# A long convolution beside an attention: pair products made by GpSimd in the loop of the first attention, half of the query products on GpSimd, expert weights loaded in the convolution

## The reference, cut to what matters

```python
x = x + _L0_attn_ref(_layernorm(x, axis=-1), ...)
x = x + _L0_xattn_ref(ctx_2048, ctx_2048, _layernorm(x, axis=-1), L0_xattn_ssm_kernel, L0_xattn_D, 8)
x = x + _L0_ffn_ref(...)        # mixture of experts
...
def _L0_xattn_ref(k, v, q, ssm_kernel, D, head_dim):
    ...
    kv = jnp.einsum('bhil,bhjl->bijhl', k_, v_)
    kv_f = jnp.fft.rfft(kv, n=fft_size)
    kernel_f = jnp.fft.rfft(ssm_kernel, n=fft_size)
    y = jnp.fft.irfft(kv_f * kernel_f, n=fft_size)[..., :L]
    out = y + kv * D[None, None, None, :, None]
    out = jnp.einsum('bijhl,bhil->bjhl', out, q_)
```

## Time and profile before

| | us |
|---|---|
| median of 3 runs | 718.73 (716.68 to 723.39) |
| the profiled execution | 719.01 |
| its span, first to last instruction | 716.8 |
| first attention, tiles 6 to 13 | 8.95 for each tile (two in 17.91) |
| convolution, VectorE's first product to the end of its last sum | 172.84 to 246.19, 73.35 |

### The profile page before, as it was taken

How to read it: one execution, slowest core, us unless ns; L and a number is a source line. 1 busy time by engine, 2 the same in 40 slices (tenths; PEclk the granted TensorE clock), 3 DMA queues, 4 the chain that set the end, 5 groups by cost and what they waited for, 6 DMA issues and landing times.

```text
span 716.8 us, 16348 instructions
## 1 busy us (share of the span) xinstructions
PE 611.1 (85%) x4646; PEld 462.3 (65%) x4647; DVE 535.8 (75%) x1217; ACT 389.6 (54%) x796; POOL 320.4 (45%) x672
## 2 busy tenths in 40 slices
PE   6999999987888899988999777999999577637776
PEld 5788888864444575566777566888888433225554
DVE  4789999975999985324222688999999668689994
ACT  2667777762111133144332264777777458869993
POOL 1223222254999443611111554333333368566772
PEclk9999999999999999999999998999999869959999
DMA  8912400001333000274541212000000000000001
GB/s 293 416 61 64 139 0 0 0 2 21 57 56 57 15 1 15 104 243 126 156 129 51 59 39 111 2 1 0 0 0 2 2 0 0 0 0 1 32 29 59
DMA packets 27343, 42.00 MB, mean 59 GB/s; under 512 B 3521, under 2 KB 22609, under 8 KB 26401
## 3 DMA queue, kind: packets, MB, share of 16 engines
q1 hardware_dynamic: 23808, 31.14, 14.5%
q0 software_dynamic: 3488, 10.28, 4.2%
HBM read 31.15 MB, written 10.26 MB: 58 GB/s over the span
## 4 chain that ended last, share of the span: by engine, by line
PE 44%; DVE 18%; issue 18%; ACT 7%; POOL 5%; DMA 4%; DVEq 1%; SPq 1%; POOLq 0%; ACTq 0%
PE ps L1121 5%; PE ps L325 4%; PE ps L710 4%; PE ps L353 4%; DVE work L542 3%; PE ps L363 3%; DVE work L548 2%; PE ps L1129 2%; PE ps L373 2%; PE ps L335 2%; DVE wide L557 2%; POOL sorted_x L1182 2%; PE ps L314 2%; DMA small<-hank 2%; ACT work L1716 2%
## 5 line engine op out<-in xcount | busy, mean ns | idle before, releaser
L230 POOL TENSOR_TENSOR var_eps<-mv,powers 128x1 f32<-128x1 f32 x80 | 16.9, 211 | 199.1 <-DVE mv L221 199.1
L470 ACT COPY wide<-ps 128x512 f32<-128x512 f32 x128 | 75.6, 593 | 44.9 <-PE ps L325 42.8
L542 DVE TENSOR_REDUCE work<-ps 128x8 f32<-128x1024 f32 x64 | 77.8, 1216 | 7.1 <-PE ps L314 6.5
L325 PE MATMUL ps<-ident,work 128*128 128x128 f32 x512 | 76.8, 283 | 6.0 <-DVE work L571 3.9
L465 ACT ACTIVATE work<-work 128x1024 f32<-128x1024 f32 x64 | 68.4, 1068 | 23.2 <-DVE work L548 22.7
L548 DVE TENSOR_TENSOR work<-ps,work 128x1024 f32<-128x1024 f32 x64 | 77.8, 1216 | 0.6
L325 PEld LDWEIGHTS ps<-ident,work 128*128 128x128 f32 x512 | 59.8, 145 | 22.8 <-issue 16.7
L710 PE MATMUL ps<-ctxT,small 128*128 128x512 f32 (+1 forms) x192 | 65.3, 492 | 8.1 <-DMA small<-hank 3.0
L710 PEld LDWEIGHTS ps<-ctxT,small 128*128 128x128 f32 x192 | 35.3, 190 | 37.5 <-issue 28.5
L1155 DVE TENSOR_TENSOR work<-work,ps 128x256 f32<-128x256 f32 x23 | 9.7, 421 | 57.2 <-ACT work L1149 57.1
L353 PE MATMUL ps<-xnT,w_qkv 128*128 128x128 f32 x256 | 38.3, 296 | 16.5 <-DVE work L548 14.4
(11 more groups left out here) (207 smaller groups left out, 1553.3 us busy)
## 6 DMA issues: line engine op xcount, KB each, us to landing
wide<-in_expert_gu SPq DMA_DIRECT2D x1, 4096.0 KB, 22.3
small<-hank SPq DMA_DIRECT2D x32, 128.0 KB, 3.8
sorted_x<-small POOLq DMA_DIRECT2D x1, 2944.0 KB, 12.0
work<-sorted_x SPq DMA_DIRECT2D x23, 128.0 KB, 2.1
sorted_y<-work POOLq DMA_DIRECT2D x23, 128.0 KB, 2.2
xn_all<-in_ctx_rev_t SPq DMA_DIRECT2D x1, 2048.0 KB, 10.6
wide<-in_expert_d SPq DMA_DIRECT2D x1, 2048.0 KB, 26.5
xn_all<-in_ffn_w SPq DMA_DIRECT2D x2, 1024.0 KB, 6.3
```

Source lines behind the costliest of these rows:

```text
L325: mm = pe.transpose(T[r % 2][:, h * P:(h + 1) * P], prob[r][:, h * P:(h + 1) * P], ident)
L470: act.copy(probT[r], T[r % 2]).then_inc(s["pT"], 1)
L542: dve.tensor_reduce(mxs[:, 8 * g:8 * g + 8], S2[g], AX.X, ALU.max).then_inc(s["mx"], 1)
```

## The change: what it does

1. The pair products of a head are made by two instructions for both halves together (128x1024 and 128x512) in place of four (two 128x512, two 128x256).
2. Eleven of the 16 heads get them during the first attention: head 10 in body 5, heads 9 to 2 in bodies 6 to 13 (`"ahead"`, first thing in GpSimd's body), heads 0 and 1 in bodies 14 and 15 as before. They lie in the part of `wide` that held expert weights, in `ctx_sb` and in `ctxT`. The other five (11 to 15) are made in the convolution, after heads 1, 3, 5, 7 and 11.
3. ScalarE copies the mirrored quarter and the lower part out of PSUM (two copies for each half), and GpSimd multiplies both with the queries in one 128x512 instruction (`pool_rest`). VectorE's 128x256 product (line 816) goes; its 128x512 product and its sum stay.
4. The Toeplitz matrices have four buffers in place of two.
5. The expert weights are loaded by SP in the convolution: the first 4 MB once 12 heads are through TensorE and the load of the last Toeplitz matrix is issued, the other 2 MB after 15 heads. The wait of TensorE for them moves behind routing and shared experts.

```diff
@@ pool_body
+                if layer == 0:
+                    follow("pool", pool, t, u, "ahead")
                 if there(t):
                     pool.wait_ge(f.xn, f.base + t + 1)
...
+        AGAIN = {11: 0, 12: 1, 13: 2, 14: 3, 15: 10}
...
+            in_wide = lambda n: wide[:, n * KV:(n + 1) * KV]
+            kv = {0: ctxT[:, 0:KV], 1: ctxT[:, 2048:2048 + KV], 10: ctx_sb[:, 2048:2048 + KV]}
+            kv.update({h: in_wide(9 - h) for h in range(2, 10)})
+            kv.update({h: kv[free] for h, free in AGAIN.items()})
...
+                if name == "pool" and step == "ahead" and not isinstance(t, int):
+                    pool_pairs(eng, 15 - t, wide[:, ds((t - 6) * KV, KT * UPPER)],
+                               wide[:, ds((t - 6) * KV + KT * UPPER, KT * LOWER)])
@@ sync
+                with sp.Fori(1, CH // 4) as i:
+                    for k in range(4):
+                        h = 4 * i + k
+                        sp.wait_ge(s["conv"], 4 * (h - 3))
+                        load_toep(sp, h, k)
...
+                sp.wait_ge(s["conv"], 4 * 10)
+                sp.dma_start(w_ex_gu, cp(a["expert_gu"])).then_inc(moe_loaded, 16)
+                sp.wait_ge(s["conv"], 4 * 15)
+                sp.dma_start(w_ex_d, cp(a["expert_d"])).then_inc(moe_loaded, 16)
@@ scalar
+                act.copy(into[:, :, :, 0:LO], upper[:, :, LO:CD, :]).then_inc(s["rest_sb"], 1)
+                act.wait_ge(s["conv"], 4 * h + 2 * lt + 2)
+                act.copy(into[:, :, :, LO:CD], lower).then_inc(s["rest_sb"], 1)
@@ gpsimd
+            def pool_early(pool, t):
+                head = {5: 10, NB - 2: 0, NB - 1: 1}
+                if t in head:
+                    pool_kv(pool, head[t])
...
+            def pool_rest(pool, h, lt):
+
+                pool.wait_ge(s["rest_sb"], 4 * h + 2 * lt + 2)
+                pool.wait_ge(s["sum"], 2 * h + lt + 1)
+                pool.tensor_tensor(products(lt)[:, :, LO:CD, :],
...
             def gpsimd(pool):
+                late = {1: 11, 3: 12, 5: 13, 7: 14, 11: 15}
                 pool.wait_ge(f.xnT, f.base_T + NB)
+                for h in range(CH):
+                    pool_rest(pool, h, 0)
+                    pool_rest(pool, h, 1)
+                    if h in late:
+                        pool.wait_ge(s["conv"], 4 * (AGAIN[late[h]] + 1))
+                        pool_kv(pool, late[h])
@@ dve_prod
-                dve.wait_ge(s["conv"], 4 * h + 2 * lt + 2)
-                dve.tensor_tensor(products(lt)[:, :, LO:CD, LO:CD],
...
```

More of the change, by code:

```diff
@@ L660, in convolution @@
             s = {k: sem(f"conv_{k}") for k in (
-                "toep0", "toep1", "kv", "conv", "quarter_sb", "quarter", "prod", "sum")}
+                "toep0", "toep1", "toep2", "toep3", "kv", "conv", "rest_sb", "rest", "prod", "sum")}
             LO = CD // 2
             UPPER, LOWER = NB * LO * CD, NB * LO * LO
-            kv = [kt_x(ctxT[:, u * 2048:u * 2048 + KT * (UPPER + LOWER)], UPPER + LOWER) for u in range(2)]
-            quarter = [xnT[:, lt * D:(lt + 1) * D] for lt in range(2)]
+            KV = KT * (UPPER + LOWER)
+            rest = [xnT, xn]
+            in_wide = lambda n: wide[:, n * KV:(n + 1) * KV]
+            kv = {0: ctxT[:, 0:KV], 1: ctxT[:, 2048:2048 + KV], 10: ctx_sb[:, 2048:2048 + KV]}
+            kv.update({h: in_wide(9 - h) for h in range(2, 10)})
+            kv.update({h: kv[free] for h, free in AGAIN.items()})
             toep = [kt_x(small[:, 800 + u * 512:800 + (u + 1) * 512], D) for u in range(2)]
+            toep += [kt_x(w_qkv[0][:, u * 512:(u + 1) * 512], D) for u in range(2)]
             prod = [ctx_sb[:, u * 1024:(u + 1) * 1024] for u in range(2)]
@@ L676, in beside @@
                         front_xn(eng, f, n, 1 - u)
-                if name == "pool" and there(n):
+                if name == "pool" and step == 0 and there(n):
                     front_rstd(eng, f, n, 1 - u)
+                if name == "pool" and step == "ahead" and not isinstance(t, int):
+                    pool_pairs(eng, 15 - t, wide[:, ds((t - 6) * KV, KT * UPPER)],
+                               wide[:, ds((t - 6) * KV + KT * UPPER, KT * LOWER)])
                 if name == "pe" and step == 0 and there(m):
@@ L729, in tensor, with act_rest @@
                 pe.wait_ge(s["toep1"], 32)
[L730 removed]
                 pe_blocks(pe, 1, range(4))
[L732 to L742 removed]
+                for h in range(2, CH):
+                    pe.wait_ge(s[f"toep{h % 4}"], 32 * (h // 4 + 1))
+                    pe.wait_ge(s["kv"], 2 * (max(10, h) + 1))
+                    for lt in range(2):
+                        pe.wait_ge(s["prod"], 2 * (h - 2) + lt + 1)
+                        pe.wait_ge(s["rest_sb"], 4 * (h - 2) + 2 * lt + 2)
+                        pe_blocks(pe, h, (2 * lt, 2 * lt + 1))
+            def act_rest(act, h, u, lt):
+                into = rest[lt].rearrange("p (b i j) -> p b i j", i=LO, j=CD)
+                upper = ps[4 * u + 2 * lt].rearrange("p (b j i) -> p b i j", j=LO, i=CD)
+                lower = ps[4 * u + 2 * lt + 1][:, 0:LOWER].rearrange("p (b i j) -> p b i j", i=LO, j=LO)
                 act.wait_ge(s["conv"], 4 * h + 2 * lt + 1)
                 if not isinstance(h, int) or h > 0:
[L746 to L749 removed]
+                    act.wait_ge(s["rest"], 2 * (h - 1) + lt + 1)
+                act.copy(into[:, :, :, 0:LO], upper[:, :, LO:CD, :]).then_inc(s["rest_sb"], 1)
+                act.wait_ge(s["conv"], 4 * h + 2 * lt + 2)
+                act.copy(into[:, :, :, LO:CD], lower).then_inc(s["rest_sb"], 1)
             def scalar(act):
@@ L806, in gpsimd @@
-                for h in range(CH - 2, CH):
-                    for lt in range(2):
-                        pool_quarter(pool, h, lt)
+                for h in range(CH):
[4 more added lines that the diff above has]
+                        pool_kv(pool, late[h])
             def dve_prod(dve, h, u, lt):
-                q = queries(lt)
                 dve.wait_ge(s["sum"], 2 * h + lt + 1)
-                dve.wait_ge(s["conv"], 4 * h + 2 * lt + 2)
@@ L822, in dve_prod @@
                                   ps[4 * u + 2 * lt].rearrange("p (b i j) -> p b i j", i=LO, j=CD),
-                                  q[:, :, ds(h * CD, CD)].unsqueeze(2).broadcast_to([P, NB, LO, CD]),
+                                  queries(lt)[:, :, ds(h * CD, CD)].unsqueeze(2).broadcast_to([P, NB, LO, CD]),
                                   ALU.mult).then_inc(s["prod"], 1)
@@ L827, in dve_sum @@
                 dst = outT3[:, lt, :].rearrange("p (b n) -> p b n", n=P)
-                dve.wait_ge(s["prod"], 4 * h + 2 * lt + 2)
-                dve.wait_ge(s["quarter"], 2 * h + lt + 1)
+                dve.wait_ge(s["prod"], 2 * h + lt + 1)
+                dve.wait_ge(s["rest"], 2 * h + lt + 1)
                 dve.tensor_reduce(dst[:, :, ds(h * CD, CD)], products(lt),
@@ L1936, in first_stores @@
                 work[t](eng)
-            if name == "pool" and t in (NB - 2, NB - 1):
-                conv.early[1](eng, t - NB + 2)
+            if name == "pool":
+                conv.early[1](eng, t)
             if name == "pe":
```

101 lines of the change are left out of this document (35 added, 66 removed).

## The result

| | before | after |
|---|---|---|
| median, us (20 runs each) | 721.96 (715.17 to 728.79) | 725.94 (722.65 to 729.61) |
| profiled execution, us | 719.01 | 726.56 |
| its span, us | 716.8 | 724.8 |
| VectorE's first product of the convolution, us | 172.84 | 183.32 |
| end of its last sum, us | 246.19 | 252.10 |

The ratio on record is 1.0073, with an interval of 1.0053 to 1.0093: slower by 0.7%, inside what the prediction called no change. The prediction was 725.0.

A forecast was written before the change was run, and what follows sets the result against it. VectorE and TensorE were taken as both full in the attention loop, VectorE as leading the convolution. Profiled 719.01 + 10.9 (attention) - 4.7 (convolution) = 725.2, said as 725.0 us since that execution lies 0.3 above the median; range 713 to 732.

The forecast's parts named there:

- no change: Whole kernel: a measured time of 711.5 to 725.9 us, about 1% either way, chance 0.54.
- Part 1, cause: Attention: VectorE's line 242 stands still while the GpSimd instruction begun just before it runs, ending 0.15 us after it.
- Part 1, bodies 7 to 12: Attention loop: pair products at VectorE's back in place of the bias cost +1.1 us in each body, 6.6 us.
- line 242 at 0.4: Attention loop: line 242 staying at 0.4 or 0.8 us, not about 2.0, would show the forecast wrong.
- VectorE comes first: Attention: GpSimd late by 0.1 us, line 242 takes 0.41, 0.36 less in seven bodies; 711.7 us; chance 0.09.
- Body 6: Attention: head 10's pair products delay the factor of tile 8, and line 242 then waits; +2.6 us once.
- the third rival, TensorE's clock: Attention: stalls lower TensorE's clock once or some times, adding 2 to 6 us, 727 to 731; chance 0.10.
- the tail: Attention bodies 14 and 15: the instruction beside line 242 grows from 1.04 to 1.89 us, +0.85 each, +1.7.
- Parts 3 and 4: Convolution: VectorE's half 1.96 us in place of 2.29, GpSimd's rest product 1.3; 68.6 us in all, -4.7 us.
- the stall: Convolution: VectorE stands about 1.0 us behind each of five heads, for GpSimd's rest and pair products; 5 us.
- TensorE as its bound, 66: Convolution: with the rest product at 1.07 us, TensorE limits the stage to 66 us; 722.5 in all; chance 0.15.
- Part 5: Expert weights loaded during the convolution land more than 30 us before their first use and cost nothing.

The follow-up runs named there:

- e1: Changed kernel with the 128x512 pair product ahead of the 128x1024 one in the attention; 719.73 us, ratio 0.9999.
- e2: Changed kernel with all pair products of the attention moved behind the bias in GpSimd's body; 722.24 us, ratio 1.0004.
- e8: Changed kernel with a 128x1 GpSimd addition ahead of the two pair products in the loop; one execution, 738.66 us.
- e3: Kernel before the change, with pair products of eight heads made a second time in the attention loop, into unread columns; 730.29 us, ratio 1.0137.
- e4: Changed kernel with only head 10's pair products moved, to behind the bias of body 5; 728.84 us, ratio 1.0126.
- e6: Changed kernel with the pair products of heads 11 to 15 cut into three 128x512 instructions behind three rest products; 732.47 us, ratio 0.9982.
- e5: Changed kernel with the attention's pair products behind the bias and head 10's moved to GpSimd's body 3; 729.01 us, ratio 0.992.
- e9: e2 with GpSimd's DMA issue moved one body later, head 10 kept in place; single execution, 715.94 us.
- e10: e2 with head 10's pair products one body earlier, behind the bias that follows a 16x1 addition; single execution, 720.9 us.

## Why the prediction was right, and where two errors met

**The sum was right: 725.0 against 725.94.** The profiles give +5.9 us up to the end of the convolution, where the sum had +6.2. That the time itself is hit within 1 us is in part luck. The base had been the median of three runs, 718.73, and over 20 runs it is 721.96, 3.2 higher; the medians lie 4.0 us apart (the ratio on record stands for 5.3) where 6.2 were predicted. The two nearly cancel. The profiled executions lie 7.6 us apart, with 2.1 us behind the convolution, where nothing was predicted.

**Part 1, cause: right.** Line 242 is held for the whole of the GpSimd instruction beside it and ends 0.15 us after it. e1 changes the cost by changing the length, e2 removes it by changing the neighbour. The price of the pair products, worked out from a 0.19 fixed part, was exact: 1.88 to 1.89 and 1.03 to 1.04 where nothing disturbs them (the long one takes 1.96 to 2.02 where VectorE went first).

**Part 1, bodies 7 to 12: mis-sized, 6.6 against 3.4.** The held bodies cost 1.02 to 1.04 (taken: 1.1), but they are three and not six. The prediction had named line 242 at 0.4 as a sign that it was wrong, and in bodies 7, 9 and 11 that is what stands there. The rival "VectorE comes first" had the condition right (GpSimd late by 0.1) and was given to all bodies or none. The pair product that GpSimd's next body opens with is one turn of the hardware loop further on behind bodies 7, 9 and 11, and there GpSimd idles 0.18 to 0.24 us on "issue"; behind 8, 10 and 12 it is in the same turn and there is no such row. That the turn's border delays it fits the parity in the changed kernel, e1 and e8, but it is argued and not shown: no run unrolled the loop. The border alone can't be it. In the kernel before the bias follows the factor across it without a pause (84.43 + 0.55 and 84.99 in body 7), in e8 the small addition does so too, and in e3 the product is only 0.08 and 0.09 late in bodies 9 and 11 and holds VectorE. Why a pair product is late there stays open. The bodies that escape gain nothing against the kernel before (+0.07 to +0.14), although line 242 is 0.4 shorter: VectorE then waits 0.39 us for TensorE's scores (line 314) ahead of the next maxima. The rival's price of -0.36 for each body was wrong for that reason.

**Body 6: 2.6 against 3.8.** The late factor (1.24) and the collision (1.17) are 2.4, as worked out. The rest is the third rival, TensorE's clock, which got a chance of 0.10 as a case of its own. It came to 1.38 there and 0.88 in body 15, 2.3 us in all. Where the clock stays at 1.00 the excess is gone: in e4, with the same collision and a stand of 1.38 us, and in e8, with both late factor and collision and a stand of 2.91 us. In the tail 1.7 was predicted and 2.6 measured, of which 0.84 + 0.85 are the collisions. I named 2.6 us of standing in the prediction and priced only the standing. That a stand of this length brings the slow clock on was right in the changed kernel and e6 and wrong in e8; what decides it is not shown.

So the attention came to 9.8 us by the wrong two terms, 3.2 too much in the loop and 2.1 too little for the clock, where 10.9 was predicted; 0.7 more came from before the changed stretch.

**Parts 3 and 4: right.** The convolution took 68.78 (68.6), a half 1.96 (1.96), the rest product 1.27 (1.3), the stall 1.18 five times (1.0), the start 0.94 in all. e6 takes the stalls away and nothing else takes their place until 63.6. The rival "TensorE as its bound, 66" was wrong in its floor.

**Part 5: right.** The expert weights land 60 us before their use.

## What to carry to other kernels

An engine that looks half idle is not free at every place in its queue: the GpSimd instruction that begins just before a VectorE instruction like line 242 (`tensor_scalar`) costs its own length, so put a short instruction there and the long one behind it (here the swap of e1 was worth 0.7%, and e5, with the bias there and head 10 moved, 1.5%). A stall that is added to an otherwise full loop can cost more than itself, for behind it TensorE may come back at half its clock; look at the granted clock behind it in several executions, since one of 2.91 us did no such harm here and ones of 1.76 and 2.62 did. And work that is moved off the leading engine only helps as evenly as it is spread: five stalls of 1.2 us went when the same products were cut in three.

## What the runs showed that I had not expected

- A VectorE instruction that begins beside GpSimd's DMA issue (0.55 us) is kept out for 4.22 us, through the issue and three instructions in sequence behind it (e2, e4); the same three without the issue hold it through the bias only, 0.81 (e9) and, with a small addition ahead, 0.95 (e10). The Trainium skill, SBUF — State Buffer, section "Who interferes with whom", tells of an exclusion for one instruction at a time; e1 agrees with it, and body 4 of e2 goes beyond it. Why the issue matters stays open.
- The tie: VectorE's start in the trace 0.05 us (e3) and 0.08 us (the bias in body 3) ahead of GpSimd's still lost, 0.11 ahead won.
- TensorE's granted clock behind a stand in a full loop: 1.00 after 1.38 us (e4), 0.57 after 1.76 (e1), 0.50 after 2.62 (the changed kernel) and 3.54 (e2), but 1.00 again after 2.91 (e8), and 0.50 in the tail of e1 after 1.11. The length of the stand alone does not order them, and what does stays open.
